# A gated cross-attention and mixing layer in fp32 on one core: batch loops written out, register waits made constant, spacing instructions removed

## The chip, the core and the metric

The kernel runs on one core of one Trainium2 chip, as one program for the five engines: TensorE (PE), VectorE (DVE), ScalarE (ACT), GpSimd (POOL) and SyncE (SP), which issues all transfers. The engines run by themselves and meet at semaphores. The metric is the device time of one execution in microseconds (us), less is better. In the profile PE is a matmul, PEld the load of its weights, and an engine's name with a q behind it (DVEq) is its sequencer, which handles waits, register operations and branches.

## What is computed

```python
x = x + tanh(g_xattn) * attention(layernorm(x), ctx, ctx, mask, q, k, v, o weights and biases)
x = x + tanh(g_ffn)   * mix(layernorm(x), W_r, W_k, W_v, mu_r, mu_k)

# attention: Q = q @ q_w.T + q_b, K and V likewise from ctx, 16 heads of 32
#   scores = Q K^T / sqrt(32), masked keys to -1e9, softmax, times V, then @ o_w.T + o_b
# mix: x_prev is x shifted by one row; xr = mu_r*x + (1-mu_r)*x_prev, xk likewise
#   out = sigmoid(xr @ W_r.T) * (square(relu(xk @ W_k.T)) @ W_v.T)
```

There are 8 batches of 512 rows by 512 channels, all in fp32; `ctx` has the same shape.

## The kernel before

Precision: a projection splits both operands into a high and a low part and adds three products (low by high, high by low, high by high). The scores put the parts of Q and K on top of each other in 96 rows, which SyncE copies together for every group, with 12 transfers of 64 KB for Q and 12 for K (`stack_q`, `stack_k`).

Stage 1 is attention, written to DRAM as `ctx_dram`. A batch has four groups of four heads; a group has 16 tiles of 128 query rows by 512 keys. For one tile TensorE makes the scores, VectorE adds the mask and finds the row's extreme in one custom operation (`mask_and_min`, to `neg_s` and `negmax`, line 875), ScalarE takes the exponential (`exp`, to `probs`, line 697), TensorE transposes it in four blocks (line 525), and VectorE and ScalarE copy the result out by turns (`probs_out`, to `pT`). At a group's end 32 matmuls multiply by V (`context`, line 537), and the result is scaled by the denominators into `ctx_sb` (side item R, line 865). Between the tiles TensorE does parts of the projections that the next groups need (`PE_SIDE`). This order is written out by hand in tables; each engine has its own list, shifted by a few steps. VectorE and ScalarE begin the next batch's first three tile steps (`early_steps`) at the end of their loop body. So their jump back comes after the third step of a batch's first group, in the middle of the tile work, and on VectorE right behind `ctx_sb`.

Each engine has a loop over batches 0 to 6 (`Fori(0, B - 1)`), and batch 7 is written out behind it, since it leaves out what a next batch needs and takes up the first steps of stage 2. Within the loop a semaphore's target depends on the batch, so it is computed into a register, and the wait compares with that register. Before and behind the loop the same Python functions get a number and give constants.

Stage 2 takes a unit of 256 rows per step, 16 units in all, in a loop over batches with two steps per turn; the last batch is again written out. TensorE's order in a step is: K projection, R projection, the next unit's eight `xh` transposes (line 591), V projection, next output projection. VectorE forms `x` (first residual), the statistics `mv` (line 985), `mix_r_lo` (line 1021), `kact` and, when ScalarE has `kact_hi`, `kact_lo` (line 1036), and then the two normalised halves `xh` (line 992). GpSimd forms the inverse root of the variance, a chain of 15 operations of 128x2 elements, each waiting for the one before (`inverse_root`, lines 1088 to 1095, through `link`), then adds the output bias to the next input (`add_bias`, `x_in`, line 1114), then adds the residual to the result (`o_sb`, line 1130). The same chain serves the first norm (`normalise`), where its first run stands at the start of the kernel.

`apart(engine)` increments a semaphore that nobody reads. It stands between a wait and the instruction behind it at the mask step, the aggregation of the statistics, every link of GpSimd's chain, and at SyncE's waits. In the compiled program the wait then sits on this increment, and the operation behind it carries none:

```python
def link(ins):
    n[0] += 1
    ins.then_inc(sem_, 1)
    pool.wait_ge(sem_, base + n[0])
    apart(pool)
```

Of the kernel before, what the change touches and what calls it, by code (L numbers as in the profile page):

```python
# [26 lines left out]
B, S, D = 8, 512, 512  # L27
# [89 lines left out]
def build(nc, x, ctxT, mask, g_xattn, g_ffn, wq, bq, wk, bk, wv, bv, wo, bo, wr, wkk, wvv, mur, muk, ident_d, out,  # L117
# [11 lines left out]
    with keep:  # L129
# [79 lines left out]
        small_ld, bias_ld, bv_ld = sem("small_ld"), sem("bias_ld"), sem("bv_ld")  # L209
        unused = sem("unused")  # L210
        ident_ld = sem("ident_ld")
# [80 lines left out]

        def apart(engine):


            engine.sem_inc(unused, 1)

        CHAIN = 3 + 4 * NEWTON
# [5 lines left out]
        def _(sp):  # L304
# [43 lines left out]
            def stack_q(b, n, heads):  # L348
                sp.wait_ge(side_hi, q_hi_count(b, n))
                apart(sp)  # L350
                stack_rows("Q", n, (0, 1), qk_hi[0], heads)
                sp.wait_ge(side_done, q_lo_count(b, n))
                apart(sp)
                stack_rows("Q", n, (2,), qk_lo[0], heads)

            def stack_k(b, n, heads):
                sp.wait_ge(side_done, done(side_no(b, ("K", n))))
                apart(sp)
                for j in heads:
                    stack_rows("K", n, (0, 2), qk_hi[1], (j,))  # L360
                    stack_rows("K", n, (1,), qk_lo[1], (j,))
# [28 lines left out]
            def store_context(b, c):  # L390
                sp.wait_ge(side_done, done(side_no(b, ("R", c))))
                apart(sp)
                sp.dma_start(ctx_dram[bass.ds(b * D + c * P, P), :], ctx_sb[:, c % 2, :]).then_inc(ctx_st[c % 2], 16)

            def batch(b):
                for c in range(GROUPS):
                    if c == 0 and not is_last(b):


                        sp.wait_ge(side_done, done(b * SIDE_PER_BATCH + len(PROLOGUE) - 1))  # L400
                        apart(sp)
                        load_x(b + 1)
                    if c:
                        store_context(b, c - 1)
                    if not (is_last(b) and c == GROUPS - 1):

                        sp.wait_ge(s_mm, tile_no(b, c, 0) + HEAD)
                        apart(sp)
                        if is_last(b) and c == GROUPS - 2:

                            sp.wait_ge(side_mm, mm_no(b, ("Q", c + 1)) + 1)
                            apart(sp)
                            load_w2(0)
                        stack_group(b, c + 1)
                    if c == 0 and not is_last(b):
                        load_ctx(b + 1)
                    if is_last(b) and c == GROUPS - 2:

                        load_unit(0, 0)
                        load_w2(1)  # L420
                        load_unit(0, 1)
                        load_w2(2)
                        load_w2(3)
                store_context(b, GROUPS - 1)

            with sp.Fori(0, B - 1) as b:
                batch(b)
# [6 lines left out]
            def step2(b, h):  # L434
                if not is_last(b):
                    sp.wait_ge(c2_lo, b * 2 + h + 1)
                    apart(sp)
                    sp.wait_ge(x1_done, (b * 2 + h + 1) * UM)
                    apart(sp)
                    load_unit(b + 1, h)  # L440
                sp.wait_ge(o_done, b * 2 + h + 1 + HEAD)
                apart(sp)
                sp.dma_start(out[bass.ds(b * S + h * UNIT, UNIT), :].rearrange("(m p) c -> p m c", p=P),
                             o_sb[:, h]).then_inc(out_st[h], 16)

            with sp.Fori(0, B - 1) as b:
                step2(b, 0)
                step2(b, 1)
# [7 lines left out]
        def _(pe):  # L456
# [136 lines left out]

            with pe.Fori(0, B - 1) as b:
                batch(b)
# [52 lines left out]

            with pe.Fori(0, B - 1) as b:
                step2(b, 0)  # L650
                step2(b, 1)
# [5 lines left out]
        def _(act):  # L657
# [72 lines left out]
            def early_steps(b):  # L730

                for i in range(EARLY):
                    tile_step(b, 0, i)
                    if i == HI_STEP and not isinstance(b, int):
                        side(b - 1, "R", GROUPS - 1)
# [31 lines left out]
            early_steps(0)  # L767
            with act.Fori(0, B - 1) as b:
                batch(b)
# [42 lines left out]
            mixed_hi(0, 0, 1)  # L812
            with act.Fori(0, B - 1) as b:
                step2(b, 0)
                step2(b, 1)
# [5 lines left out]
        def _(dve):  # L821
# [12 lines left out]
            def mean_and_variance(b):  # L834
                dve.wait_ge(xhat_done, b * TT)
                for t in range(TT):
                    dve.wait_ge(bn_done, b * TT + t + 1)
                    apart(dve)
                    nc.vector.bn_aggr(mv[:, t, :], stats[:, t, :]).then_inc(mv_done, 1)  # L839
# [28 lines left out]
            def mask_and_min(b, c, i):  # L868
# [4 lines left out]
                dve.wait_ge(p_exp, tile_no(b, c, i) + 1)  # L873
                apart(dve)
                nc.vector.tensor_tensor_reduce(neg_s[:, i % SM_RING, :], s_bank[i % S_BANKS][:], mask_big[:, q, :], 1.0,  # L875
# [52 lines left out]
            def early_steps(b):  # L928

                for i in range(EARLY):  # L930
                    tile_step(b, 0, i)
                    if i == LO_STEP and not isinstance(b, int):
                        side(b - 1, "R", GROUPS - 1)
# [31 lines left out]
            def residual1(b, h):  # L965
# [16 lines left out]
                for m in range(UM):  # L982
                    dve.wait_ge(bn2_done, u * UM + m + 1)
                    apart(dve)
                    nc.vector.bn_aggr(mv2[:, m, :], stats2[:, m, :]).then_inc(mv2_done, 1)
# [9 lines left out]
            early_steps(0)  # L995
            with dve.Fori(0, B - 1) as b:
                batch(b)
# [63 lines left out]
            mixed_lo(0, 0, 0)  # L1061
            with dve.Fori(0, B - 1) as b:
                step2(b, 0)
                step2(b, 1)
# [5 lines left out]
        def _(pool):  # L1070
# [7 lines left out]
            def inverse_root(base, sem_, var, ve, y, t):  # L1078
# [3 lines left out]
                def link(ins):  # L1082
                    n[0] += 1
                    ins.then_inc(sem_, 1)
                    pool.wait_ge(sem_, base + n[0])
                    apart(pool)

# [9 lines left out]
            def normalise(b):  # L1097
                pool.wait_ge(mv_done, (b + 1) * TT)
                apart(pool)
                inverse_root(b * CHAIN, pool_chain, mv[:, :, 1], var_eps[:], rstd[:], newton[:])  # L1100
                if isinstance(b, int):
                    return
# [4 lines left out]
            normalise(0)  # L1107
            with pool.Fori(0, B - 1) as b:
                normalise(b + 1)
# [7 lines left out]
            def inverse_root2(b, h):  # L1117
                u = b * 2 + h
                pool.wait_ge(mv2_done, (u + 1) * UM)
                apart(pool)  # L1120
                inverse_root(u * CHAIN, pool_chain2, mv2[:, :, 1], var_eps2[:], rstd2[:], newton2[:])
# [20 lines left out]
            split_w2(3)  # L1142
            with pool.Fori(0, B - 1) as b:
                step2(b, 0)
                step2(b, 1)
# [41 lines left out]
```

## Time and profile before

| | us |
|---|---|
| three timed runs | 1279.31, 1281.83, 1282.83 |
| median | 1281.83 |
| profiled execution, first to last instruction (span) | 1275.5 |
| TensorE matmuls busy | 1184.9 (93%) |
| VectorE busy | 956.5 (75%) |
| ScalarE busy | 763.2 (60%) |
| GpSimd busy | 253.7 (20%) |

For the profiled execution the page gives the span alone; the timed runs' median is 6.3 us above it. The page shares the busy time out over 40 slices, but an average over slices says little here: the two stages have different limits, and the interesting places are short. The rows below are therefore mostly of single stretches. In a row of windows each engine has its busy us and, in brackets, its count of instructions; PEclk is the granted TensorE clock as a share of full speed (1.00 is 2.4 GHz, half is 1.2 GHz).

### The profile page before, as it was taken

Reading aid. Unit: us, or ns where it says so; the run is one execution under the profiler, and the core shown is the slowest. Engines: PE = TensorE matmul, PEld = TensorE weight load, DVE = VectorE, ACT = ScalarE, POOL = GpSimd, SP = SyncE. Lnnn points to the kernel's source line nnn. Section 1 sums busy time; section 2 is a strip of 40 time slices with the busy share of each in tenths; the row PEclk is TensorE's granted clock in tenths of the full one; section 3 lists DMA queues with packets and bytes.
Section 4 is the critical chain, followed back from the end, with each engine's and each line's share of the span. In section 5 each row is a group of like instructions: output and inputs, shape, how many; then the busy total and the mean of one; then the engine's idle time right before and its main releaser. Section 6 shows DMA issues by size and latency. Waiting matters only on the chain.

```text
span 1275.5 us, 25860 instructions
## 1 busy us (share of the span) xinstructions
PE 1184.9 (93%) x7424; PEld 933.5 (73%) x7424; DVE 956.5 (75%) x2011; ACT 763.2 (60%) x1632; POOL 253.7 (20%) x427
## 2 busy tenths in 40 slices
PE   3999899999999989999999999987999999999997
PEld 3777676777767767777676777765878878878886
DVE  5778688688778867868877887879677677777763
ACT  4678677678768867867866886774432433343332
POOL 1030030030012003003002100025433443343441
PEclk9999999999999989999998999987999999999999
DMA  6433332253243343233224332461111211211200
GB/s 216 113 96 80 100 108 61 70 143 79 64 125 89 79 98 91 76 99 106 75 59 134 82 83 59 115 196 52 51 50 64 84 49 49 99 49 49 78 37 34
DMA packets 72685, 109.81 MB, mean 86 GB/s; under 512 B 14864, under 2 KB 23696, under 8 KB 72592
## 3 DMA queue, kind: packets, MB, share of 16 engines
q1 hardware_dynamic: 72592, 108.92, 29.9%
q14 instruction: 77, 0.63, 0.2%
q8 instruction: 16, 0.26, 0.1%
HBM read 41.76 MB, written 16.78 MB: 46 GB/s over the span
## 4 chain that ended last, share of the span: by engine, by line
PE 65%; DVE 12%; issue 12%; POOL 6%; ACT 1%; POOLq 1%; DMA 1%; DVEq 1%; SPq 1%; ACTq 0%
PE bank L525 15%; PE bank L461 14%; PE bank L492 11%; PE bank L537 9%; PE bank L518 8%; PE bank L501 6%; DVE xh L992 3%; POOL newton L1094 2%; DVE neg_s L875 2%; PE bank L507 1%; POOL var_eps L1088 1%; DVE stats L832 1%; DVE pT L881 1%; DVE stats L981 1%; POOL rstd L1095 1%
## 5 line engine op out<-in xcount | busy, mean ns | idle before, releaser
L697 ACT ACTIVATE probs<-neg_s,negmax 128x512 f32<-128x512 f32 x512 | 368.3, 721 | 58.6 <-DVE negmax L875 50.5
L875 DVE CUSTOM_DVE_ANT_0 neg_s<-bank,mask_big 128x512 f32<-128x512 f32 x512 | 346.4, 684 | 63.7 <-PE bank L518 36.0
L525 PE MATMUL bank<-ident,probs 128*128 128x128 f32 x2048 | 320.7, 280 | 21.8 <-ACT probs L697 21.3
L525 PEld LDWEIGHTS bank<-ident,probs 128*128 128x128 f32 x2048 | 245.0, 143 | 82.5 <-ACT probs L697 43.0
L518 PE MATMUL bank<-k_stack,q_stack 96*128 96x512 f32 x512 | 247.8, 484 | 15.3 <-DVE negmax L875 15.3
L881 DVE COPY pT<-bank 128x512 f32<-128x512 f32 x256 | 176.5, 690 | 105.8 <-PE bank L525 104.6
L704 ACT COPY pT<-bank 128x512 f32<-128x512 f32 x256 | 149.2, 583 | 107.9 <-PE bank L525 104.1
L1088 POOL TENSOR_SCALAR var_eps<-mv 128x2 f32<-128x2 f32 (+1 forms) x24 | 16.6, 690 | 661.7 <-DVE mv L839 597.5
L537 PE MATMUL bank<-pT,v_sb 128*32 128x512 f32 x1024 | 118.8, 605 | 0.8 <-issue 0.5
L518 PEld LDWEIGHTS bank<-k_stack,q_stack 96*128 96x128 f32 x512 | 99.5, 195 | 22.3 <-DVE negmax L875 10.8
L697 ACT ACTIVATION_READ_ACCUMULATOR probs<-neg_s,negmax 128x1 f32 x512 | 97.0, 190 | 0.0
L537 PEld LDWEIGHTS bank<-pT,v_sb 128*32 128x32 f32 x1024 | 33.2, 111 | 70.1 <-issue 70.1
L795 ACT ACTIVATE relu<-bank 128x512 f32<-128x512 f32 x32 | 19.2, 599 | 90.0 <-PE bank L461 89.9
L1114 POOL TENSOR_TENSOR x_in<-x_in,tgbo 128x1024 f32<-128x1024 f32 x16 | 41.2, 2578 | 140.4 <-DMA x_in<-x 137.2
L1130 POOL TENSOR_TENSOR o_sb<-o_sb,x 128x1024 f32<-128x1024 f32 x16 | 39.1, 2445 | 146.8 <-DVE o_sb L1051 146.8
L1104 POOL TENSOR_SCALAR x_rows<-x_rows,mv,rstd 128x512 f32<-128x512 f32 x28 | 57.9, 2078 | 1.5 <-POOL rstd L1095 1.5
L688 ACT COPY ctx_sb<-bank 128x512 f32<-128x512 f32 x32 | 18.8, 588 | 62.6 <-PE bank L507 62.6
L492 PE MATMUL bank<-cT_lo,wk_hi 128*128 128x512 f32 x128 | 40.4, 418 | 16.6 <-DVE cT_lo L853 16.6
L992 DVE TENSOR_SCALAR xh<-x,mv,rstd 128x512 f32<-128x512 f32 x32 | 49.2, 1580 | 7.1 <-POOL rstd L1095 7.0
L975 DVE SCALAR_TENSOR_TENSOR x<-bank,tg,x_in 128x512 f32<-128x512 f32 x32 | 23.4, 750 | 36.9 <-POOL o_sb L1130 36.8
L1033 DVE SCALAR_TENSOR_TENSOR kact<-bank,relu 128x512 f32<-128x512 f32 x32 | 22.1, 692 | 35.5 <-ACT relu L795 35.5
L501 PE MATMUL bank<-wv_hi,cT_lo 128*128 128x256 f32 x256 | 47.4, 292 | 0.0
(111 smaller groups left out, 2169.5 us busy)
## 6 DMA issues: line engine op xcount, KB each, us to landing
k_stack<-k_hi SPq DMA_DIRECT2D x256, 64.0 KB, 2.0
q_stack<-q_hi SPq DMA_DIRECT2D x256, 64.0 KB, 2.0
x_rows<-x SPq DMA_DIRECT2D x8, 1024.0 KB, 6.9
cT_raw<-ctxT SPq DMA_DIRECT2D x8, 1024.0 KB, 5.5
k_stack<-k_lo SPq DMA_DIRECT2D x128, 64.0 KB, 2.0
q_stack<-q_lo SPq DMA_DIRECT2D x128, 64.0 KB, 2.0
ctx_dram<-ctx_sb SPq DMA_DIRECT2D x32, 256.0 KB, 2.1
c_raw<-ctx_dram SPq DMA_DIRECT2D x16, 512.0 KB, 4.2
```

The source lines that it names most:

```text
L461: mm = nc.tensor.matmul(dst, lhs(left, a), rhs(right, a), start=(part == 0 and a == 0), stop=(part == TERMS - 1 and a == CH - 1))
L492: mm = nc.tensor.matmul(bank[:], left[:, at % CH, cols], right[:, at % CH, :], start=(at == 0), stop=(at == TERMS * CH - 1))
L501: mm = nc.tensor.matmul(bank[:, k * UNIT:(k + 1) * UNIT], left[:, a, keys * P:(keys + 1) * P], right[:, a, n // 2 * UNIT:(n // 2 + 1) * UNIT],
L518: nc.tensor.matmul(s_bank[i % S_BANKS][:], stack[slot][0][:, j, q * P:(q + 1) * P], stack[slot][1][:, j, :], start=True, stop=True).then_i ...
L525: mm = nc.tensor.transpose(pt_bank[i % 2][:, a * P:(a + 1) * P], probs[:, i % P_RING, a * P:(a + 1) * P], ident[:])
L537: nc.tensor.matmul(pv_bank[j * HD:(j + 1) * HD, :], v_sb[:, a, head * HD:(head + 1) * HD], pT[:, j, a, :], start=(a == 0), stop=(a == TT - 1))
L697: nc.scalar.activation(probs[:, i % P_RING, :], neg_s[:, i % SM_RING, :], ACT.Exp, bias=negmax[:, k:k + 1], scale=-1.0, accum_out=den[:, g ...
L704: nc.scalar.copy(pT[:, j, :, q * P:(q + 1) * P], blocks(pt_bank[i % 2])).then_inc(pt_out[1], 1)
L875: nc.vector.tensor_tensor_reduce(neg_s[:, i % SM_RING, :], s_bank[i % S_BANKS][:], mask_big[:, q, :], 1.0, 3e38, ALU.add, ALU.min, negmax[ ...
L881: nc.vector.tensor_copy(pT[:, j, :, q * P:(q + 1) * P], blocks(pt_bank[i % 2])).then_inc(pt_out[0], 1)
L992: nc.vector.tensor_scalar(xh[:, m], x1[:, h, m], mv2[:, m, 0:1], rstd2[:, m:m + 1], ALU.subtract, ALU.mult).then_inc(xh_done, 1)
L1104: nc.gpsimd.tensor_scalar(x_rows[:, t, :], x_rows[:, t, :], mv[:, t, 0:1], rstd[:, t:t + 1], ALU.subtract, ALU.mult).then_inc(xhat_done, 1)
```

## The change

All ten loops become Python loops, so every batch stands as straight code in each engine's program. With that every wait compares with a constant. `apart` and its semaphore go, at all its places. The order of operations, their operands and their semaphores stay. The two tests for "inside the loop" (`not isinstance(b, int)`) become tests on the batch number.

```diff
-        unused = sem("unused")
...
-        def apart(engine):
-            engine.sem_inc(unused, 1)
...
             def store_context(b, c):
                 sp.wait_ge(side_done, done(side_no(b, ("R", c))))
-                apart(sp)
...
-            with sp.Fori(0, B - 1) as b:
+            for b in range(B - 1):
                 batch(b)
             batch(B - 1)
...
-            with pe.Fori(0, B - 1) as b:
+            for b in range(B - 1):
                 step2(b, 0)
                 step2(b, 1)
...
                 for i in range(EARLY):
                     tile_step(b, 0, i)
-                    if i == LO_STEP and not isinstance(b, int):
+                    if i == LO_STEP and b:
                         side(b - 1, "R", GROUPS - 1)
...
                 dve.wait_ge(s_mm, tile_no(b, c, i) + 1 + HEAD)
                 dve.wait_ge(p_exp, tile_no(b, c, i) + 1)
-                apart(dve)
                 nc.vector.tensor_tensor_reduce(neg_s[:, i % SM_RING, :], s_bank[i % S_BANKS][:], mask_big[:, q, :], 1.0,
                                                3e38, ALU.add, ALU.min, negmax[:, k:k + 1]).then_inc(s_min, 1)
...
                     n[0] += 1
                     ins.then_inc(sem_, 1)
                     pool.wait_ge(sem_, base + n[0])
-                    apart(pool)
...
             def normalise(b):
                 pool.wait_ge(mv_done, (b + 1) * TT)
-                apart(pool)
                 inverse_root(b * CHAIN, pool_chain, mv[:, :, 1], var_eps[:], rstd[:], newton[:])
-                if isinstance(b, int):
+                if b == 0:
                     return
```

## Rows read from the trace of the kernel before

**Rows 1.** Windows from a batch's last context product to the next's first, first and seventh.

```profile
137.75:167.76 30.01, 26.46 (x168) 19.85 (x172) 20.32 (x52) 18.41 (x44) 0.16 (x1) 0.94 0.40 107
...
766.68:790.77 24.09, 23.80 (x168) 18.43 (x172) 18.31 (x47) 17.83 (x44) 0.00 (x0) 1.00 0.24 64
sum 204.97, PE 184.47 PEld 138.84 DVE 139.83 ACT 128.53 POOL 0.94; mean PE 26.35 PEld 19.83 DVE 19.98 ACT 18.36 POOL 0.13
```

**Rows 2.** Windows: batch 0's first and second groups, batch 7's first.

```profile
63.08:86.64 23.56, 23.56 (x169) 18.18 (x172) 19.03 (x50) 17.93 (x44) 11.32 (x19) 1.00 0.39 113
86.64:111.43 24.79, 23.58 (x157) 16.83 (x157) 20.29 (x50) 19.84 (x48) 0.00 (x0) 1.00 0.29 76
...
790.77:814.29 23.52, 23.52 (x168) 18.18 (x172) 18.45 (x47) 17.90 (x44) 0.00 (x0) 1.00 0.34 87
```

**Rows 3.** The chain of waits at the first jump back: start, us, what.

```profile
146.83 1.89 issue
...
149.77 1.78 issue
```

**Rows 4.** Timeline of VectorE: behind the first jump, and at the fall-through.

```profile
149.07 0.69 DVE L875 CUSTOM_DVE_ANT_0 neg_s<-bank,mask_big 128x512 f32<-128x512 f32 x1 [2.24 <-ACT probs L697]
...
775.68 0.68 DVE L875 CUSTOM_DVE_ANT_0 neg_s<-bank,mask_big 128x512 f32<-128x512 f32 x1
```

**Rows 5.** Instruction fetches (packets, MB): from 140 to 160, whole run, 790.77 to 814.29.

```profile
q14 instruction: 6, 0.05, 1.2%
...
q8 instruction: 16, 0.26, 0.1%
...
q8 instruction: 1, 0.02, 0.3%
```

**Rows 6.** The page, busy time of TensorE: matmuls and weight loads.

```profile
PE 1184.9 (93%) x7424; PEld 933.5 (73%) x7424; DVE 956.5 (75%) x2011; ACT 763.2 (60%) x1632; POOL 253.7 (20%) x427
```

**Rows 7.** Windows: one step of stage 2.

```profile
1049.70:1074.30 24.60, 23.29 (x130) 19.89 (x129) 17.70 (x26) 7.46 (x10) 9.75 (x17) 1.00 0.20 64
```

**Rows 8.** Waits of the whole run: us in total, times, longest.

```profile
PE bank L591 <- DVE xh L992: 21.4, 15, 3.5
```

**Rows 9.** Timeline of VectorE and GpSimd in one step of stage 2.

```profile
1056.04 1.40 DVE L1051 SCALAR_TENSOR_TENSOR o_sb<-bank,tg,recept 128x512 f32<-128x512 f32 x2
...
1057.52 2.39 POOL L1130 TENSOR_TENSOR o_sb<-o_sb,x 128x1024 f32<-128x1024 f32 x1 [8.80 <-DVE o_sb L1051]
...
1062.98 1.19 DVE L1021 TENSOR_TENSOR mix_r_lo<-mix_r,mix_r_hi 128x1024 fp32r<-128x1024 f32 x1
1063.26 0.99 POOL L1088 TENSOR_SCALAR var_eps<-mv 128x2 f32<-128x2 f32 x1 [3.35 <-DVE mv L985]
...
1065.93 0.19 POOL L1094 TENSOR_SCALAR newton<-newton 128x2 f32<-128x2 f32 x1 [0.20 <-POOL newton L1093]
...
1068.90 1.23 DVE L1036 TENSOR_TENSOR kact_lo<-kact,kact_hi 128x1024 fp32r<-128x1024 f32 x1 [1.12 <-ACT kact_hi L797]
1068.95 1.23 POOL L1094 TENSOR_SCALAR newton<-newton 128x2 f32<-128x2 f32 x1 [0.20 <-POOL newton L1093]
...
1070.59 3.06 DVE L992 TENSOR_SCALAR xh<-x,mv,rstd 128x512 f32<-128x512 f32 x2 [0.46 <-POOL rstd L1095]
...
1070.73 2.63 POOL L1114 TENSOR_TENSOR x_in<-x_in,tgbo 128x1024 f32<-128x1024 f32 x1 [0.18 <-POOL rstd L1095]
```

**Rows 10.** Timeline of the start: GpSimd's first chain, waits on constants.

```profile
11.70 0.20 POOL L1093 TENSOR_TENSOR newton<-newton,var_eps 128x4 f32<-128x4 f32 x1 [0.18 <-POOL newton L1092]
12.10 2.00 POOL L1094 TENSOR_SCALAR newton<-newton 128x4 f32<-128x4 f32 x1 [0.20 <-POOL newton L1093]
...
18.44 1.92 DVE L902 TENSOR_SCALAR x_rows<-x_rows,mv,rstd 128x512 f32<-128x512 f32 x4 [1.99 <-POOL rstd L1095]
```

**Rows 11.** Timeline: `xh` with GpSimd idle, and GpSimd's W_r split.

```profile
1242.96 1.01 DVE L992 TENSOR_SCALAR xh<-x,mv,rstd 128x512 f32<-128x512 f32 x2 [0.47 <-POOL rstd L1095]
...
868.77 4.78 POOL L1134 TENSOR_TENSOR w2r_lo<-w_raw,w2r_hi 128x2048 fp32r<-128x2048 f32 x1 [0.18 <-POOL rstd L1095]
```

More of the change, by code:

```diff
@@ L349, in stack_q @@
                 sp.wait_ge(side_hi, q_hi_count(b, n))
-                apart(sp)
                 stack_rows("Q", n, (0, 1), qk_hi[0], heads)
                 sp.wait_ge(side_done, q_lo_count(b, n))
-                apart(sp)
                 stack_rows("Q", n, (2,), qk_lo[0], heads)
@@ L357, in stack_k @@
                 sp.wait_ge(side_done, done(side_no(b, ("K", n))))
-                apart(sp)
                 for j in heads:
@@ L391, in store_context @@
                 sp.wait_ge(side_done, done(side_no(b, ("R", c))))
-                apart(sp)
                 sp.dma_start(ctx_dram[bass.ds(b * D + c * P, P), :], ctx_sb[:, c % 2, :]).then_inc(ctx_st[c % 2], 16)
@@ L400, in batch @@
                         sp.wait_ge(side_done, done(b * SIDE_PER_BATCH + len(PROLOGUE) - 1))
-                        apart(sp)
                         load_x(b + 1)
@@ L407, in batch @@
                         sp.wait_ge(s_mm, tile_no(b, c, 0) + HEAD)
-                        apart(sp)
                         if is_last(b) and c == GROUPS - 2:
                             sp.wait_ge(side_mm, mm_no(b, ("Q", c + 1)) + 1)
-                            apart(sp)
                             load_w2(0)
@@ L436, in step2 @@
                     sp.wait_ge(c2_lo, b * 2 + h + 1)
-                    apart(sp)
                     sp.wait_ge(x1_done, (b * 2 + h + 1) * UM)
-                    apart(sp)
                     load_unit(b + 1, h)
                 sp.wait_ge(o_done, b * 2 + h + 1 + HEAD)
-                apart(sp)
                 sp.dma_start(out[bass.ds(b * S + h * UNIT, UNIT), :].rearrange("(m p) c -> p m c", p=P),
                              o_sb[:, h]).then_inc(out_st[h], 16)
-            with sp.Fori(0, B - 1) as b:
+            for b in range(B - 1):
                 step2(b, 0)
@@ L592, in transposes @@
                     mm.then_inc(t_mm, 1)
-            with pe.Fori(0, B - 1) as b:
+            for b in range(B - 1):
                 batch(b)
@@ L647, in step2 @@
                     o_proj(b + 1, h)
-            with pe.Fori(0, B - 1) as b:
+            for b in range(B - 1):
                 step2(b, 0)
@@ L733, in early_steps @@
                     tile_step(b, 0, i)
-                    if i == HI_STEP and not isinstance(b, int):
+                    if i == HI_STEP and b:
                         side(b - 1, "R", GROUPS - 1)
@@ L767, in _ @@
             early_steps(0)
-            with act.Fori(0, B - 1) as b:
+            for b in range(B - 1):
                 batch(b)
@@ L812, in _ @@
             mixed_hi(0, 0, 1)
-            with act.Fori(0, B - 1) as b:
+            for b in range(B - 1):
                 step2(b, 0)
@@ L873, in mask_and_min @@
                 dve.wait_ge(p_exp, tile_no(b, c, i) + 1)
-                apart(dve)
                 nc.vector.tensor_tensor_reduce(neg_s[:, i % SM_RING, :], s_bank[i % S_BANKS][:], mask_big[:, q, :], 1.0,
@@ L983, in residual1 @@
                     dve.wait_ge(bn2_done, u * UM + m + 1)
-                    apart(dve)
                     nc.vector.bn_aggr(mv2[:, m, :], stats2[:, m, :]).then_inc(mv2_done, 1)
@@ L995, in _ @@
             early_steps(0)
-            with dve.Fori(0, B - 1) as b:
+            for b in range(B - 1):
                 batch(b)
@@ L1061, in _ @@
             mixed_lo(0, 0, 0)
-            with dve.Fori(0, B - 1) as b:
+            for b in range(B - 1):
                 step2(b, 0)
@@ L1107, in _ @@
             normalise(0)
-            with pool.Fori(0, B - 1) as b:
+            for b in range(B - 1):
                 normalise(b + 1)
@@ L1119, in inverse_root2 @@
                 pool.wait_ge(mv2_done, (u + 1) * UM)
-                apart(pool)
                 inverse_root(u * CHAIN, pool_chain2, mv2[:, :, 1], var_eps2[:], rstd2[:], newton2[:])
@@ L1142, in _ @@
             split_w2(3)
-            with pool.Fori(0, B - 1) as b:
+            for b in range(B - 1):
                 step2(b, 0)
```

## The prediction

> **What bounds the kernel now.** I read the stretches by stage first, then the idle time inside them, then the chain of waits. In stage 1 (attention, to about 880 us) TensorE sets the pace: from one context product to the next, in the first head group of a batch, it is busy 23.56 of 23.56 us [rows 2]. The reader should see two exceptions. The first is the step from a batch's last group into the next batch's first. It takes 30.01 us at the first of six such places, but 24.09 us at the seventh, where the loop falls through instead of jumping back [rows 1]. In the chain of waits the jump shows as two holes with no releaser, 1.89 and 1.78 us, right behind VectorE's `ctx_sb` product, which is the last operation of its loop body [rows 3]. VectorE's next mask step then starts after 2.24 us of idle, and with it TensorE's next scores, while at the fall-through the mask step follows `ctx_sb` directly [rows 4]. The second exception is the second group, 24.79 us for 23.58 us of TensorE work [rows 2].
>
> In stage 2 one step (256 rows) takes 24.60 us with TensorE busy 23.29 [rows 7]. What it lacks is the second pair of `xh` transposes: 15 waits for VectorE's `xh`, 21.4 us in all, of which one is 3.5 us at the stage change, so 14 of 1.28 us [rows 8]. `xh` waits for GpSimd's inverse root, a chain of 15 tiny operations.
>
> **The change part by part.**
>
> *Jumps back, stage 1.* Seven rows of one pattern, 204.97 us in all; without the fall-through's 24.09 that is 180.88 us for six, against 6 x 24.09 = 144.54 [rows 1]. Difference 36.3 us. Straight code has only fall-throughs, so all of it goes. Part of it is clock: the granted clock is 0.94 in the first of these stretches and 1.00 in the fall-through's; it goes with the holes, as TensorE no longer idles there. Against the comparison: the seventh stretch has no statistics and no loads for a further batch. But the first group of batch 0 has both and still runs at 23.56 [rows 2]. I allow 30 to 37 us.
>
> The Trainium skill, "Runtime: NRT & Kernel Launch", section on instruction fetch, says a taken branch outside the present window of pages must fetch its target first, while straight code is streamed ahead. The trace agrees: six fetch packets of q14 in the 20 us around a jump [rows 5], and the holes beside them. By that page too the whole 36.3 us would go.
>
> *Jumps back, stage 2.* No step with a jump is longer than one without (the chain repeats every 24.6 us), so I count nothing. Here the chain through GpSimd and TensorE's queue covers the jump; if that cover went, a hole of 1.8 us times six would show, but the jump goes as well.
>
> *Constant instead of register waits.* TensorE's first group in the straight last batch takes 23.52 us, in the loop 23.56 [rows 2]: 0.04 us. GpSimd's chain at the start waits on constants, with the spacing, and has the same 0.18 us between operations as in the loop [rows 9, 10]. Nothing, therefore; at most 0.04 x 32 groups = 1.3 us.
>
> *Spacing instructions, stage 2.* This takes the most work. With spacing an operation of the chain starts 0.18 to 0.20 us after the one before and lasts 0.19 [rows 9, 10]. A GpSimd operation that waits directly starts sooner: `o_sb` ends on VectorE at 1057.44 and starts on GpSimd at 1057.52, 0.08 us [rows 9]. So a link goes from 0.375 to 0.27 us. The bounds are 0.18 (no gain) and 0.03 us of gap; I take 0.08, the row of the same engine.
>
> The chain doesn't run free, though. Its first operation is 0.99 us long, from 1063.26 to 1064.25, and ends just behind VectorE's `mix_r_lo` (to 1064.17); the fourteenth is 1.23 us long and ends just behind `kact_lo` (1068.90 to 1070.13) [rows 9]. These two VectorE operations keep GpSimd out. The other way round, the two `xh` together take 1.01 us where GpSimd is idle and 3.06 us where it adds the bias to `x_in` [rows 9, 11]. After the change the start of the chain is not earlier (`mix_r_lo` holds it), and 14 links of 0.27 end at 1064.25 + 3.78 = 1068.03. Before, it was 1070.56. That is before `kact_lo` wants to start. But GpSimd goes straight on to `x_in`: 1068.11, 2.39 us long as the `o_sb` add of the same size, with VectorE free again 0.21 us before its recorded end (the second `xh` takes half of 1.01 us and ends at 1073.65, so it began at 1073.15, while `x_in` ends at 1073.36). So `kact_lo` runs not from 1068.90 but from 1070.29, to 1071.52, and the two `xh` end at 1072.53 instead of 1073.65. A step gains 1.12 us; its cap is TensorE's idle 24.60 - 23.29 = 1.31. Times 14: 15.7 us. With a gap of 0.03 the add is out of the way early enough for the full 1.31: 18.3 us. With 0.14 or more `x_in` and `kact_lo` are ready together near 1068.9, and whichever comes first `xh` ends near 1073.3: 0.3 us, 4.6 in all.
>
> The rule of the Trainium skill on this is in "SBUF — State Buffer", section "Who interferes with whom": VectorE and GpSimd share one port pair, the instruction that starts first holds it to its end, and the other is blocked fully. The rows above agree. A sum without that rule would give the step 14 x 0.105 = 1.47 us on the chain, capped at 1.31.
>
> *Spacing, stage 1.* VectorE's mask step loses one instruction between its wait and its start. Where TensorE is full this is worth nothing, and it is hidden by TensorE's own work. In the second group TensorE idles 24.79 - 23.58 = 1.21 us [rows 2]; eight batches make 9.7 us at most. No row shows what share is latency; I take a third, 3.2 us, bounds 0 and 9.7. SyncE's spacing costs nothing: its queue waits for others.
>
> *Start and stage change.* The first chain reaches VectorE's `x_rows` at 18.44 us after 1.99 us of idle. Its sixth operation was held 2.00 us by the split of the K weights [rows 10]; six faster links before it and eight behind would bring about 1.0 us, but `k_lo` needs the K product, which TensorE finishes as before. I take 0.8 (0 to 1.5). At the stage change GpSimd's split of W_r (4.78 us) begins at 868.77, right behind its chain and with the two `xh` under way, and holds the second of them [rows 11]. Starting 1.4 us earlier it ends earlier, but now gets in front of both. I take 0.5 gained, bounds -3 and +4, since half-clock stretches lie here too.
>
> *Sum.* 36.3 + 15.7 + 3.2 + 0.8 + 0.5 = 56.5 us. From the profiled execution's span of 1275.5 that is 1219.0. The timed runs lie 6.3 us above this span (median 1281.83), so 1225.3; I say 1225.
>
> **The rivals.**
>
> A. *The bias add eats the gain.* The chain is quicker, but the gap stays above 0.14 us, or `x_in` and `kact_lo` meet badly: stage 2 gives 4 instead of 16. For it: 3.06 against 1.01 us of `xh`. Against it: 0.08 us at `o_sb`. 1225 + 12 = 1237 us.
>
> B. *TensorE becomes the bound of stage 2.* The links shrink to 0.22 us, as `xh` itself starts 0.03 us behind `rstd`. 18.3 instead of 15.7, and more of the 9.7 in stage 1: 1219 us.
>
> C. *Straight code has holes of its own in VectorE or ScalarE*, fewer than the jumps: half of 36.3 stays: 1243 us. Against it: in the last batch's first group, straight code already, a fetch arrives while TensorE is busy 23.52 of 23.52 us [rows 2, 5].
>
> D. *Slower: TensorE has to fetch.* Its loop body stays in its instruction memory: q8 shows 16 fetches in the whole run [rows 5] for 14,848 TensorE instructions, matmuls and weight loads [rows 6]. Written out, it must fetch steadily. In the straight first group of the last batch there is one fetch for 340 instructions [rows 2, 5], which makes 44 over the kernel. It decides from 56.5 / 44 = 1.3 us of stall per fetch; at the price of VectorE's second hole, 1.78 us, it costs 78 us against 56.5: 1304 us. Against it stands that same group: its fetch cost TensorE nothing, as it was busy throughout. The skill's page on the runtime calls such a crossing mostly hidden.
>
> E. *Nothing changes*, because unrolling only moves the holes: 1282 us.
>
> **How the numbers follow.** Forecast 0.60, A 0.15, B 0.13, C 0.06, D 0.04, E 0.02. The forecast's own range is 1218 to 1232. For 8 in 10 I add B wholly and most of A, and the bounds of the stage change: 1214 to 1240. A measurement can tell about 0.3%, 4 us, from no change. Faster 0.94, the same 0.02 (E), slower 0.04 (D).
>
> **What would show it.** Right: all seven group steps of rows 1 near 24.1 us at clock 1.00, no hole near 1.8 us on VectorE; GpSimd's links near 0.27 us; `x_in` before `kact_lo`, and `kact_lo` late by about 1.4 us against its release; stage 2 steps of 23.5 us; q8 above 40 fetches, without idle TensorE. Wrong: steps of 23.3 us (B) or above 24.2 (A), links still at 0.37, group steps spread between 25 and 30 us (C), or TensorE idle with no releaser at regular distances (D).

## The result, and the profile after

The changed kernel takes 1233.6 us (median of 4 runs, 1232.1 to 1236.2) against 1281.7 for the kernel before (4 runs). The ratio is 0.963, interval 0.961 to 0.965. The profiled execution has a span of 1230.8 us against 1275.5, so the spans differ by 44.7 us where the prediction had 56.5. Its own time is 1232.7, 1.9 us above its span, and in every other run of this study whose span is on record the time is 1.7 to 2.0 us above it.

The page after, busy time and the two kinds of instruction fetch, answers to [rows 5, 6]:

```profile
PE 1167.7 (95%) x7424; PEld 921.5 (75%) x7424; DVE 942.5 (77%) x2011; ACT 745.2 (61%) x1619; POOL 237.4 (19%) x427
...
q8 instruction: 61, 1.00, 0.3%
q14 instruction: 50, 0.41, 0.1%
```

The seven windows from a batch's last context product to the next batch's first (first, second, third, fifth and seventh shown; columns as in [rows 1]):

```profile
136.30:161.57 25.27, 24.49 (x168) 18.51 (x172) 20.18 (x52) 18.08 (x44) 0.23 (x2) 1.00 0.40 108
236.24:261.02 24.78, 24.13 (x168) 18.48 (x172) 20.07 (x52) 18.08 (x44) 0.23 (x1) 1.00 0.41 108
335.70:361.46 25.76, 24.49 (x168) 18.51 (x172) 20.18 (x52) 18.07 (x44) 0.23 (x2) 1.00 0.42 111
...
535.89:561.89 26.00, 24.49 (x168) 18.51 (x172) 20.17 (x52) 18.08 (x44) 0.23 (x2) 1.00 0.43 107
...
736.68:760.80 24.12, 23.83 (x168) 18.45 (x172) 18.30 (x47) 17.87 (x44) 0.00 (x0) 1.00 0.26 68
sum 176.38, PE 170.29 PEld 129.47 DVE 139.22 ACT 126.33 POOL 1.37; mean PE 24.33 PEld 18.50 DVE 19.89 ACT 18.05 POOL 0.20
```

The clock is 1.00 everywhere and no step is near 30 us any more. But the first six, 152.26 us together, don't reach the seventh's 24.12: 7.5 us are left over six steps (6 x 24.12 = 144.72). VectorE has 52 operations in them and 47 in the seventh. TensorE's busy time in the six fell from 160.7 to 146.5 us for the same matmuls: before, the granted clock was 0.94, 1.00, 0.94, 0.89, 0.89 and 0.89 in them. At clock 1.00, in the second window, it was 25.25 us, and 6 x 25.25 is 151.5. So by this estimate some 9 of the 28.6 us gained are TensorE's own work done at the full clock. The sixth window before:

```profile
661.01:692.01 31.00, 27.63 (x168) 20.96 (x172) 20.32 (x52) 18.52 (x44) 0.16 (x1) 0.89 0.43 121
```

The following groups, in the windows that answer to [rows 2], are as they were:

```profile
61.62:85.16 23.54, 23.54 (x169) 18.20 (x172) 18.74 (x50) 17.91 (x44) 11.08 (x18) 1.00 0.39 114
85.16:109.97 24.81, 23.59 (x156) 16.86 (x157) 20.19 (x50) 19.93 (x48) 0.00 (x0) 1.00 0.30 77
```

VectorE's timeline at the first boundary answers to [rows 4]:

```profile
144.53 0.68 DVE L848 TENSOR_TENSOR ctx_sb<-bank,ctx_sb 128x512 f32<-128x512 f32 x1
145.12 0.68 DVE L857 CUSTOM_DVE_ANT_0 neg_s<-bank,mask_big 128x512 f32<-128x512 f32 x1
...
152.36 0.69 DVE L816 BATCH_NORM_STATS2 stats<-x_rows 128x6 f32<-128x512 f32 x1 [0.39 <-DMA x_rows<-x]
```

The mask step now follows `ctx_sb` directly. In its place there is a small wait, of the statistics for the next batch's `x_rows`. SyncE issues that load at 145.61 and it takes 6.73 us. VectorE waits 0.4, 0, 0.9, 0.2, 1.1 and 0.5 us for it at the six boundaries, 3.1 in all. Less its wait, each of the six takes 24.8 to 24.9 us.

One stage 2 step, windows (answers to [rows 7]), then VectorE and GpSimd in it (answers to [rows 9]), and the waits of the whole run (answer to [rows 8]):

```profile
886.53:910.05 23.52, 23.32 (x130) 19.88 (x130) 17.06 (x26) 7.47 (x10) 8.61 (x17) 1.00 0.20 65
```

```profile
889.29 0.19 POOL L1074 TENSOR_SCALAR newton<-newton 128x2 f32<-128x2 f32 x1
889.56 0.19 POOL L1075 TENSOR_TENSOR rstd<-rstd,newton 128x2 f32<-128x2 f32 x1
...
889.84 2.43 POOL L1093 TENSOR_TENSOR x_in<-x_in,tgbo 128x1024 f32<-128x1024 f32 x1
890.69 2.67 DVE L1017 TENSOR_TENSOR kact_lo<-kact,kact_hi 128x1024 fp32r<-128x1024 f32 x1 [1.12 <-ACT kact_hi L781]
893.27 0.99 DVE L973 TENSOR_SCALAR xh<-x,mv,rstd 128x512 f32<-128x512 f32 x2
...
893.95 1.06 PE L575 MATMUL bank<-ident,xh 128*128 128x128 f32 x8 [0.20 <-DVE xh L973]
...
908.18 1.19 DVE L1002 TENSOR_TENSOR mix_r_lo<-mix_r,mix_r_hi 128x1024 fp32r<-128x1024 f32 x1
908.36 1.09 POOL L1068 TENSOR_SCALAR var_eps<-mv 128x2 f32<-128x2 f32 x1 [3.18 <-DVE mv L966]
```

```profile
PE bank L575 <- DVE xh L973: 7.5, 16, 3.1
...
DVE stats L816 <- DMA x_rows<-x: 10.0, 6, 6.9
```

The links start 0.27 to 0.28 us apart, `x_in` starts before `kact_lo` is released, and `kact_lo` lasts 2.67 us instead of 1.23. TensorE's wait for `xh` has gone from 21.4 to 7.5 us. Of the 10.0 us for `x_rows`, 6.9 stand at the start of the kernel.

Where the 44.7 us of span come from:

| | before | after | gained | predicted |
|---|---|---|---|---|
| start to first context product | 63.08 | 61.62 | 1.5 | 0.8 |
| six steps across a batch boundary | 180.88 | 152.26 | 28.6 | 36.3 |
| other groups of stage 1 | | same | 0.0 | 3.2 |
| last batch's second and third group | 47.44 | 46.48 | 1.0 | |
| last batch's third context product to stage 2's first step | 63.8 | 64.2 | -0.4 | 0.5 |
| 13 steps of stage 2 | 24.62 each | 23.52 each, one 23.71 | 14.1 | 15.7 (14 steps) |

The rest of the 44.7 is rounding. The start ranges from 60.7 to 65.0 us over the profiles of this study, so its 1.5 us is no finding. Nor is the 1.0 of the last batch: its third group ran at clock 0.93 in the trace of before and took 23.92 us, while in every other run, those with loops and spacing included, it took 23.1 us or less.

### The profile page after: what moved, and what is told of

It is laid out like the page before. It is cut to its first block, busy times and chain, and to the rows that moved or that the text cites. A ratio compares the mean times of both kernels' runs of the same rounds, so it can differ in the third digit from the quotient of the medians.

```text
span 1230.8 us, 22178 instructions
## 1 busy us (share of the span) xinstructions
PE 1167.7 (95%) x7424; PEld 921.5 (75%) x7424; DVE 942.5 (77%) x2011; ACT 745.2 (61%) x1619; POOL 237.4 (19%) x427
## 4 chain that ended last, share of the span: by engine, by line
PE 76%; DVE 9%; issue 6%; ACT 4%; DMA 4%; SPq 1%; POOL 0%; POOLq 0%; ACTq 0%; DVEq 0%
PE bank L445 24%; PE bank L509 14%; PE bank L476 12%; PE bank L521 10%; PE bank L502 7%; PE bank L485 6%; DMA x_rows<-x 3%; DVE neg_s L857 3%; ACT probs L681 2%; PE bank L491 2%; PE bank L575 1%; DVE pT L863 1%; DVE xh L973 1%; DMA pT<-wkT 1%; DVE ctx_sb L848 1%
## 5 line engine op out<-in xcount | busy, mean ns | idle before, releaser
L509 PE MATMUL bank<-ident,probs 128*128 128x128 f32 x2048 | 314.8, 276 | 17.3 <-ACT probs L681 16.8
L509 PEld LDWEIGHTS bank<-ident,probs 128*128 128x128 f32 x2048 | 240.4, 141 | 75.6 <-ACT probs L681 40.7
L502 PE MATMUL bank<-k_stack,q_stack 96*128 96x512 f32 x512 | 243.3, 475 | 6.0 <-DVE negmax L857 5.9
L1017 DVE TENSOR_TENSOR kact_lo<-kact,kact_hi 128x1024 fp32r<-128x1024 f32 x16 | 40.0, 2498 | 17.9 <-ACT kact_hi L781 17.9
```

The lines of the kernel that those rows point to most:

```text
L502: nc.tensor.matmul(s_bank[i % S_BANKS][:], stack[slot][0][:, j, q * P:(q + 1) * P], stack[slot][1][:, j, :], start=True, stop=True).then_i ...
L509: mm = nc.tensor.transpose(pt_bank[i % 2][:, a * P:(a + 1) * P], probs[:, i % P_RING, a * P:(a + 1) * P], ident[:])
L1017: nc.vector.tensor_tensor(kact_lo[:].rearrange("p a t -> p (a t)"), kact[:].rearrange("p m d -> p (m d)"), kact_hi[:].rearrange("p a t -> ...
```

## The experiments

Times are medians, and each ratio is against runs of the kernel before on the same chip. "Boundary sum" is the six windows of [rows 1].

**Loops alone.** All loops written out, and with that constant waits. The spacing stays.

```diff
-            with dve.Fori(0, B - 1) as b:
+            for b in range(B - 1):
```
(and so at the other nine loops)

> All loops written out and all waits constant, but every spacing instruction kept. Theory (each half of the change has its own stage): stage 1 gains as in the changed kernel, the six steps across a batch boundary take 24.8 to 26.0 us instead of 28.5 to 31.4, 28.6 us in all; stage 2 steps stay at 24.6 us, GpSimd's links at 0.37 us. Time 1281.7 - 28.6 = 1253, within 2. Rival (constants and straight code also quicken GpSimd's chain, the spacing is nearly free): stage 2 steps of 23.5 us, 1238.

1253.6 us against 1275.1, ratio 0.982 (0.979 to 0.985). The time is the one expected, but by luck: it was reckoned from 1281.7, and on this chip the kernel before takes 1275.1, so the gain is 21.5 us and not 28.6. The boundary sum is 156.1, 24.8 us less than before, and stage 2 steps are 24.65. So the two mechanisms are separate: straight code makes the boundaries' gain, and gives nothing in stage 2. Windows, fifth and sixth boundary:

```profile
540.11:565.56 25.45, 24.48 (x168) 18.52 (x172) 20.14 (x52) 18.08 (x44) 0.15 (x1) 1.00 0.41 105
640.24:668.43 28.19, 25.79 (x168) 19.74 (x172) 19.99 (x51) 18.04 (x44) 0.00 (x0) 0.94 0.40 104
```

The sixth has no jump and still shows clock 0.94: there VectorE waited 2.4 us for `x_rows`, whose load took 8.05 us. Less the waits, the other five take 24.9 to 25.0 us, nearly as in the changed kernel, and the sixth 25.8. So this load cost 3.4 us there, 2.4 of waiting and 1.0 that goes with the lower clock. VectorE's waits for `x_rows` are 5.8 us in all here and 3.1 in the changed kernel; with that 1.0 they make up the 3.8 us by which this boundary sum (156.1) exceeds 152.3.

**GpSimd alone.** Its loops written out and the links' spacing gone, all else as before.

```diff
                     pool.wait_ge(sem_, base + n[0])
-                    apart(pool)
...
-            with pool.Fori(0, B - 1) as b:
+            for b in range(B - 1):
```

> Only GpSimd's program is changed: its loops written out and the spacing in the links of its chain removed; the other four engines keep their loops and spacing. Theory: stage 2 steps fall to 23.5 us as in the changed kernel (14 x 1.1 = 15 us), the six boundary steps of stage 1 stay between 28 and 31 us, 1266 us within 3. Rival (stage 2's gain needs the other engines' straight code too): steps above 24.3 us, 1278 or more.

1262.9 us, ratio 0.989 (0.986 to 0.992). Stage 2 steps are 23.68, so GpSimd alone brings 0.94 of the 1.10 us per step. The time is some 3 us below the one expected, from a kernel before that is 6.6 us quicker here; the gain is 12.2 us, which is 13 times 0.94. The boundary sum is 182.0 for 180.9, and the holes are still in the chain of waits (start, us, what), now even longer at the first jump than in [rows 3]:

```profile
145.69 1.98 issue
148.73 3.06 issue
```

**VectorE alone.** Only its loops written out.

> Only VectorE's two loops are written out, all spacing kept; the other engines jump back as before. Theory (the two holes at each boundary are VectorE's own jump): boundary steps of 24.8 to 26 us, 1253 us within 3, stage 2 steps 24.6. Rival (ScalarE, TensorE or SyncE jump with holes of the same kind, hidden so far behind VectorE's): boundary steps of 27 us or more, 1262 or above.

1260.0 us, ratio 0.989 (0.985 to 0.992). The boundary sum is 159.3, so VectorE's jump made 21.6 of the changed kernel's 28.6 us. Neither forecast came whole: two of the six steps are above 27 us, and the time is 7 us above the theory's. Windows of the first and second boundary, then the chain of waits at the first, and ScalarE's timeline at the second:

```profile
138.32:164.18 25.86, 24.60 (x168) 18.35 (x172) 20.21 (x52) 18.09 (x44) 0.15 (x1) 1.00 0.37 105
238.93:266.42 27.49, 24.91 (x168) 18.37 (x172) 20.32 (x52) 18.08 (x44) 0.16 (x1) 1.00 0.41 106
```

```profile
146.88 0.93 issue
```

```profile
248.55 0.72 ACT L697 ACTIVATE probs<-neg_s,negmax 128x512 f32<-128x512 f32 x1 [1.07 <-PE bank L525]
```

This hole stands on ScalarE's chain, behind its `probs`, which is where ScalarE jumps back. It is on the chain of waits at three of six boundaries; at the other three the chain runs through the transfer of `x_rows`. But ScalarE idles before this `probs` at all six, 1.06 to 1.13 us, and in the changed kernel at none. The remaining 7 us over the changed kernel can be divided by the traces. VectorE waits 3.9 us for `x_rows` here (1.6, 0.9 and 1.4 in the second, fourth and fifth window) and 3.1 in the changed kernel. Less these waits, every one of the six steps takes 25.8 to 25.9 us, against 24.8 to 24.9. So about 6.2 us, 1.0 per boundary, belong to the jumps of the other engines, which is the size of ScalarE's hole (no run writes out ScalarE's loops alone), and 0.8 to the load. SyncE issues that load 10.4 us after the context product here, and 9.3 in the changed kernel.

**Spacing back at the mask step** of the changed kernel.

```diff
                 dve.wait_ge(p_exp, tile_no(b, c, i) + 1)
+                dve.sem_inc(unused, 1)
```

> The changed kernel with the spacing put back at VectorE's mask step alone (512 times). Theory (TensorE's work hides it in the full groups): steps between context products in the loop batches as in the changed kernel to 0.05 us; batch 7's two steps, 46.48 us together, up to 1 us longer; 1232 to 1236 us. Rival (the spacing costs about 0.1 us of latency per tile wherever TensorE waits): the second-to-third and boundary steps each 0.3 us longer or more, 1238 us.

1232.2 us in a single run, span 1230.3 (changed kernel: 1230.8). The second, third and fourth groups' tiles take 23.53, 24.81 and 26.32 us, as without it. The boundary sum is 155.1 for 152.3, which by itself looks like the rival. But VectorE waits 5.8 us for `x_rows` in this run, for 3.1, and less these waits the two sums are the same to 0.1 us. So the spacing at VectorE's mask step cost nothing that this one run shows; whether it makes the load land later, one run can't tell.

**Bias add behind the output add**, in the changed kernel.

```diff
-                if not is_last(b):
-                    add_bias(b + 1, h)
                 (... o_sb add ...)
+                if not is_last(b):
+                    add_bias(b + 1, h)
```

> The changed kernel, with GpSimd's bias add x_in placed behind the o_sb add of the same step instead of in front of it, so that it runs between two VectorE operations that leave it alone (x and the statistics). Theory (the add is what holds kact_lo and costs the rest of stage 2): kact_lo back to 1.23 us from 2.67, xh done before the R projection ends, no wait at the xh transposes, steps of 23.3 us instead of 23.52, 2 to 4 us in all. Rival (TensorE's order already bounds the step): steps of 23.5 us.

1231.8 us, ratio 0.962 (0.959 to 0.965). `kact_lo` is short again. Timeline:

```profile
908.82 1.41 DVE L957 SCALAR_TENSOR_TENSOR x<-bank,tg,x_in 128x512 f32<-128x512 f32 x2 [4.94 <-POOL x_in L1093]
...
915.31 1.23 DVE L1017 TENSOR_TENSOR kact_lo<-kact,kact_hi 128x1024 fp32r<-128x1024 f32 x1 [1.11 <-ACT kact_hi L781]
```

TensorE no longer waits for `xh`, yet steps are 23.41 and 23.51 by turns, mean 23.46: a gain of 0.06 per step and not the 0.23 that the busy time of 23.29 [rows 7] would allow. The chain of waits in these steps (954.92 to 1003 us) consists of TensorE's own matmuls to 99.9%. So in this order of work TensorE bounds the step, though its busy time in it, 23.34 and 23.35 us in two neighbouring steps, is 0.07 to 0.16 less. The clash of `x_in` and `kact_lo` costs next to nothing.

**`x` loaded earlier.** The load of batch b+2's rows moves to the fourth group of batch b, in the changed kernel.

```diff
-                        sp.wait_ge(side_done, done(b * SIDE_PER_BATCH + len(PROLOGUE) - 1))
-                        load_x(b + 1)
+                        if b == 0:
+                            sp.wait_ge(side_done, done(len(PROLOGUE) - 1))
+                            load_x(1)
...
+                    if c == GROUPS - 1 and b + 2 < B:
+                        sp.wait_ge(side_done, done(side_no(b, ("T", TT - 1))))
+                        load_x(b + 2)
```

> The changed kernel, with the next x loaded in the fourth group of the batch before, right after its last transpose, instead of at the batch boundary. Theory (3.4 of the boundary steps' 7.5 us above the seventh are VectorE waiting for this transfer, the rest is the statistics' work): VectorE's statistics wait for nothing, all six boundary steps near 24.7 to 24.8 us, sum 148.4 instead of 151.8. Rival (the statistics' work alone): sum as before, 151 or more. Risk: the 1 MB transfer delays the stack copies of the fourth group, then that step grows beyond 26.33.

1230.9 us, ratio 0.961 (0.959 to 0.964). All six boundaries are now alike. Windows, the first one and the sum over six:

```profile
139.71:164.49 24.78, 24.14 (x168) 18.48 (x172) 20.07 (x52) 18.07 (x44) 0.23 (x1) 1.00 0.36 107
...
sum 148.69, PE 144.83 PEld 110.88 DVE 120.43 ACT 108.45 POOL 1.38; mean PE 24.14 PEld 18.48 DVE 20.07 ACT 18.08 POOL 0.23
```

Against the changed kernel's 152.26 that is 3.6 us: the price of waiting for `x`. The fourth group keeps its 26.33 us, so the risk named didn't come.

**Statistics one group later**, in the changed kernel.

```diff
-STATS_STEPS = (8, 10, 12, 14)
+STATS_STEPS = (1, 2, 3, 4)
...
-                        if c == 0 and i in STATS_STEPS and not is_last(b):
+                        if c == 1 and i in STATS_STEPS and not is_last(b):
```

> The changed kernel, with the four row statistics of the next x moved from the first group (tile steps 8, 10, 12, 14) to the second (1 to 4). Theory (the boundary steps' excess over the seventh is these statistics, by their own 2.8 us of VectorE and by their wait for x): six boundary steps near 24.1 us, sum 144.6 instead of 151.8; the step behind them, 23.54 us, grows by 0 to 1.2. Time 2 to 7 us below the changed kernel. Rival (a remnant of the boundary itself, such as code fetch): boundary steps stay at 24.7 or more.

1238.4 us, ratio 0.967 (0.964 to 0.970), some 5 us slower than the changed kernel where 2 to 7 us less were expected. Windows, a boundary and the group after it:

```profile
139.72:163.84 24.12, 23.83 (x168) 18.45 (x172) 18.31 (x47) 17.87 (x44) 0.00 (x0) 1.00 0.40 108
...
163.84:189.41 25.57, 24.57 (x169) 18.36 (x172) 20.92 (x55) 18.10 (x44) 11.28 (x19) 1.00 0.46 126
```

The boundary is now exactly the fall-through's 24.12. So what was left there were the statistics and the load, nothing of the jump. But where I put them they cost 2.03 us in each of seven batches, 14.2 us for the 7.9 that the boundaries gain, in a stretch where TensorE had been busy 23.54 of 23.54 us. With the bias add moved as well:

> e5 and e7 together: gains add, boundary steps near 24.1 us and stage 2 steps near 23.3, 5 to 10 us below the changed kernel. Rival: the two exchange something and the sum is less than the larger one alone.

1237.8 us, ratio 0.968 (0.965 to 0.970). Expected were 5 to 10 us below the changed kernel. Each part does what it did alone: boundary 24.13, next group 25.57, stage 2 steps 23.46.

**The changed kernel again, and the two winners together**, on one chip.

> The changed kernel once more, as the measure for the two beside it: 1230 to 1236 us, ratio to the kernel before near 0.963. Boundary steps between 24.7 and 26 us by the landing of x, stage 2 steps 23.5.

> The changed kernel with x loaded in the fourth group (as in the earlier run) and the bias add behind the o_sb add. Theory (gains add): boundary steps 24.71 each, stage 2 steps 23.46 on average, 3.4 + 0.9 = 4 us below the changed kernel. Rival: within 1 us of it.

The changed kernel: 1234.5 us, ratio 0.964 (0.962 to 0.967). The earlier load with the later bias add: 1227.4 us (1226.1 to 1228.8), ratio 0.959 (0.956 to 0.961). All its boundaries are 24.78, its stage 2 steps 23.45. It is the best version, 7.1 us under the changed kernel, where 4 were expected. The two profiles differ by 6.7: 4.0 at the boundaries as reckoned, 1.5 over the steps of stage 2 (one step of the changed kernel took 24.17 us in this profile), and 1.5 in the stretch before stage 2, whose length scatters, less 0.5 at the start. So some 2 of the 7.1 us can't be ascribed to the two edits.

**Statistics in the fourth group**, with the load in the third, and the later bias add.

```diff
-                        if c == 0 and i in STATS_STEPS and not is_last(b):
-                            row_stats(b + 1, STATS_STEPS.index(i))
+                        nxt = 1 if b == 0 and c == 0 else b + 2 if c == GROUPS - 1 else B
+                        if nxt < B and i in STATS_STEPS:
+                            row_stats(nxt, STATS_STEPS.index(i))
```

> As the former, but x is loaded in the third group behind the last transpose, and its statistics stand in the fourth group (steps 8 to 14), where VectorE is busy 21.9 of 26.3 us. Theory (the statistics cost what VectorE has no slack for): five of six boundary steps at 24.05, the fourth group's step 26.33 grows by less than 0.66, so 0 to 3 us below the former. Rival (any group with TensorE full pays for them as the second group did, 2.0 us): the fourth group's step 27 us or more, slower than the former.

1228.4 us (1227.6 to 1230.6), ratio 0.960 (0.958 to 0.963): no different from the version above, within what can be measured. Windows, the fourth group's tiles and then a boundary:

```profile
110.23:137.29 27.06, 26.72 (x188) 21.21 (x189) 23.38 (x57) 20.37 (x48) 0.10 (x1) 1.00 0.40 113
```

```profile
137.29:161.40 24.11, 23.82 (x168) 18.45 (x172) 19.11 (x50) 17.88 (x44) 11.31 (x19) 1.00 0.26 67
```

The boundary gains 0.67 and the fourth group pays 0.73 (26.33 to 27.06). The fourth group's step is above 27 us as the rival had it, but it pays 0.73 and not 2.0. The statistics cost about 0.7 us per batch in the first group and in the fourth.

## Why the prediction was right or wrong

The forecast's mechanisms held: holes of the jump and the clock with them in stage 1, the spacing in GpSimd's chain in stage 2. One of its terms was sized wrongly, and one (spacing in stage 1) had no row behind it and came to nothing. The time, 1233.6 for 1225, lies inside the range of 1214 to 1240 and just outside the forecast's own 1218 to 1232.

- **Jumps back, stage 1: the step that failed.** It stood at 36.3 and measured 28.6. The prediction compared with the fall-through, which has no statistics and no load, and set that aside with "the first group of batch 0 has both and still runs at 23.56". That is false. The window 63.08 to 86.64 starts at the *first* group's context product, so it holds the second group's tiles; the statistics and the load (issued at 43.78 us) that belong to batch 0's first group come before it. The first and the last of them in the kernel before:

```profile
53.88 0.68 DVE L832 BATCH_NORM_STATS2 stats<-x_rows 128x6 f32<-128x512 f32 x1
...
62.31 0.41 DVE L839 BATCH_NORM_AGGREGATE mv<-stats 128x2 f32<-128x6 f32 x4
```

  The name "first group" was off by one (in the whole prediction: its "second group" of 24.79 us is the third), and the control therefore controlled nothing. The row itself told it: VectorE has 52 operations in a jumping step and 47 in the fall-through, 20.32 against 18.31 us busy [rows 1]. The experiments give the missing 7.7 us: 3.6 for waiting for `x` (152.26 to 148.69), 4.0 for the statistics' work (148.69 against 6 x 24.12), the rest rounding. The jumps themselves were worth more than 28.6: with the load out of the way the sum falls from 180.88 to 148.69, by 32.2 us. Writing out the loops alone, with the spacing kept, gave 24.8, and the 3.8 between are waiting for the load and the clock that it took in one place. Most of it lay on VectorE as said; 1.0 us per boundary stays when only VectorE's loops are written out. That the clock came back holds as well (0.94 to 1.00 in the first window), and it was worth more than the first window told, since three of the six stood at 0.89.
- **What was late next** was not asked at this step. In the kernel before no statistics waited for `x_rows` at a boundary; a shorter step put the load on the path, 0 to 1.1 us each time.
- **Jumps in stage 2, constants: nothing.** Right. With all loops written out and the spacing kept, steps are 24.65 us for 24.62. One correction: with GpSimd's part alone, steps are 23.68, in the changed kernel 23.52. Once the cover of the slow chain is gone, the other engines' loops, register waits and spacing together are worth 0.16 us per step. Most of it is the spacing at VectorE's aggregation of the statistics, by the traces: its two operations take 0.42 us with GpSimd's part alone and 0.30 in the changed kernel, and `mix_r_lo`, the chain, which it holds, and `xh` come later by 0.13 to 0.15. With all loops written out and the spacing kept they take 0.41, so it isn't the loops or the registers. The prediction had no term for this. Timelines of the changed kernel and of GpSimd alone:

```profile
907.96 0.30 DVE L966 BATCH_NORM_AGGREGATE mv<-stats 128x2 f32<-128x6 f32 x2
```

```profile
938.73 0.42 DVE L985 BATCH_NORM_AGGREGATE mv<-stats 128x2 f32<-128x6 f32 x2
```

- **Spacing, stage 2: right in each link.** 0.275 per link for 0.27; `x_in` ahead of `kact_lo`; `kact_lo` done 2.67 - 1.23 = 1.44 us late for 1.4; 1.10 per step for 1.12. The Trainium skill's rule in "SBUF — State Buffer", section "Who interferes with whom", says that of two instructions that contend for the shared pair, the one issued first has it for its whole length and the other blocks. The trace agrees with the order, and nearly with the length: `kact_lo` ends 1.09 us after `x_in`, for the 1.23 that it takes alone. The total is 14.1 and not 15.7 because one of the 14 steps was the stage change, and because one step took 23.71 us. The cap, though, was wrongly read: TensorE's busy time of 23.29 isn't the least that a step can take in this order. With every wait for `xh` gone the step takes 23.46.
- **Spacing, stage 1: 3.2 for 0.** The groups are the same to 0.02 us with and without the spacing; the last batch's 1.0 us is the clock in one trace, as said above. A third of an idle time was a guess with no row behind it.
- **Start and stage change.** 1.5 for 0.8 at the start is inside its scatter. At the stage change 0.5 gained was forecast and 0.4 was lost. TensorE waits 4.47 us there (2.76 before); VectorE's `c_lo` takes 3.22 us, for 1.51 before. GpSimd's `x_in`, which waits for its transfer in both kernels, starts 0.2 us ahead of `c_lo` now and started 1.95 ahead of it before:

```profile
814.35 3.22 DVE L945 TENSOR_TENSOR c_lo<-c_raw,c_hi 128x1024 fp32r<-128x1024 f32 x1 [1.07 <-ACT c_hi L749]
...
818.31 2.04 PE L445 MATMUL bank<-w2o_lo,c_hi 128*128 128x512 f32 x4 [4.47 <-DVE ctx_sb L848]
```

  This stretch runs from 60 to 66 us over the profiles of this study; what sets it is open.
- **The time over the span.** I added 6.3 us, the distance of the median from a span. The distance is 1.9 in the changed kernel, and by that the profiled execution of before had been some 4 us quicker than the timed ones. The sum of spans was thus 11.8 us too hopeful, and this took 3.5 off the error, by luck: 1219.0 + 11.8 + 2.8 = 1233.6.
- **The rivals.** A is false (steps 23.52, not above 24.2), E too. B is false as well (steps 23.52, not 23.3; links 0.275, not 0.22); TensorE became the bound of stage 2 only with the bias add moved, at 23.46, and there was nothing to take from stage 1. C gives 1243 by a hole that isn't there: at the boundaries of the straight code neither VectorE nor ScalarE has one of that kind. D is false: 61 fetches on q8, more than the 44 reckoned, and no wait of TensorE without a releaser over 0.5 us. The page "Runtime: NRT & Kernel Launch", section "Instruction fetch mechanics", of the Trainium skill calls such crossings mostly hidden, and this trace agrees.

Two things stay open. The kernel before has a median of 1275.1 us on one chip and 1280.5 to 1281.7 on others, and its trace on that chip wasn't taken; the gain of written out loops, 21.5 us there, is measured against the quicker one. And the spacing was never removed with the loops kept on all engines, nor ScalarE's loops written out alone, so their shares rest on reading the traces.

## What to carry to other kernels

A jump back is expensive where it falls between operations that the bottleneck engine feeds on, and free where a slower chain covers it: cost it at its place, not per jump. When a stretch is compared with a "clean" one, compare the instruction counts of every engine in the two rows first, and fix from the timeline which work a window holds before giving it a name. After a stall is removed, look at once for the load that was timed to land inside it, and issue it a group earlier.

## What the runs showed of the hardware

- VectorE's jump back cost this kernel 21.6 us over six places (3.6 each, with the clock it took). Less the load's waits that took its place, it is 4.3 each. With only VectorE's loops written out, 1.0 us per place stays, and ScalarE idles 1.1 us where it jumps. TensorE's 61 fetches of straight code cost nothing that shows.
- One semaphore increment between wait and operation costs 0.10 us per link on GpSimd (0.375 to 0.275) where the links follow each other, 0.06 us each at VectorE's two aggregations (0.42 to 0.30), and nothing that shows at VectorE's mask step, where other work covers it.
- A 128x2 operation of GpSimd takes 0.19 us alone and 1.09 us beside VectorE's `mix_r_lo`; VectorE's `kact_lo` takes 1.23 us alone and 2.67 us behind a GpSimd add of 2.43 us. The delay goes both ways.
- In the one boundary step in which VectorE waited 2.4 us for a load, TensorE's granted clock was 0.94 and the step took 28.2 us, 1.0 more than the wait explains. A wait of 1.6 us in another run left the clock at 1.00. In the kernel before, with two holes in each step, five of six had 0.94 or 0.89.
